# A two-layer attention and expert kernel: score maxima run 44 units ahead in place of 64 (28 of 40 in layer 2)

## The chip, the cores and the metric

The kernel runs on one core of a Trainium2 chip. The metric is the device time of one execution in microseconds (us). A core has TensorE (PE, matmuls, with PEld for its weight loads), VectorE (DVE), ScalarE (ACT), GpSimd (POOL) and SyncE (SP, which here only issues DMAs). Each works through its own instructions in order and waits on semaphores for the others. Instructions and DMAs named here are those of the kernel's own names: `q_strip`, `k_rows`, `a_shift` and so on.

## What is computed

Two layers, each attention times a gate from a mixture of experts, over 8 batches of 512 tokens with 128 features:

```python
xn = _layernorm(x)
s = _L0_attn_ref(xn, ...)          # 16 heads of size 8, full softmax, feed-forward, layer norms
g = _silu(_L0_ffn_ref(xn, ...))    # 16 experts, one per token
x = x + s * g
xn = _layernorm(x)
s = _L1_attn_ref(xn, ...)          # 16 heads of size 8, causal, ALiBi bias
g = _silu(_L1_ffn_ref(xn, ...))    # 8 experts, two per token
x = x + s * g
```

The attention of a batch is a softmax over 512 keys for each of 16 heads and 512 queries: the row maximum is needed before the exponentials.

## The kernel before, in words

The text calls the layers 1 and 2; the code numbers them 0 and 1. There are 16 streams (batch 0 to 7 in layer 1, then batch 0 to 7 in layer 2), and the program is a sequence of **passes** numbered by the stream whose scores they compute, from -2 to 16. `plan(b)` writes out the steps of pass b once, and each of the five engines walks the same list and does its own part of every step. So the place of a step in the list is its place in every engine's queue.

**Units.** A pass consists of 64 units in layer 1 and 40 in layer 2. Unit u of pass b has two halves of work:

- a score unit of stream b: PE multiplies `k_strip` by `q_strip` (L583) into one of three banks, and ACT takes the exponential (L772, L774, L776). In layer 2 two mask matmuls come behind (L540, L541);
- a maximum unit of stream b+1: PE multiplies the other way round (L590) into one of three other banks (four in pass -1, which has no scores), and DVE reduces each row to its negated maximum (L877; in layer 2 L883, with the mask).

All maxima of stream b+1 are computed in pass b, that is a whole pass ahead. When half of them are done, the step `minus` (DVE, L905, L906) splits them into two bf16 parts, and the step `shift` brings them to where the scores need them: PE turns them (L684), ACT copies them to `a_shift` (L795), and SP writes them with four DMAs into two rows of `q_strip` (L511), so that the score matmul subtracts the maximum by itself. PE waits for these DMAs (`shift_in`) before the first score unit of either half: unit 0 and unit 32 in layer 1, unit 0 and unit 20 in layer 2.

**Places.** Between the units stand 32 places, and the tables `MISC`, `LAST0` and `EXTRA` say which other steps stand at which. The second number is the stream relative to b. `("q", 2)` and `("k", 2)` project queries and keys of stream b+2: PE (L669), ACT (L813), four POOL operations that split into three bf16 parts (L1024 to L1027), and then six DMAs on SP to `q_rows` or `k_rows` in DRAM (L482). `("fetch", 2, 0)` loads half of them back into the strips (SP, L494) and waits till the writes have landed. `load` and `loadx` are single loads on SP. `norm`, `onT`, `proj`, `yT`, `logits`, `ff1` and others use PE and the one bank for miscellaneous work; each waits till the step before it has emptied that bank (`claim`). `send0` (in `EXTRA`) writes an eighth of the tokens to the experts of layer 1: four indirect DMAs of POOL (L1662), and each `send0` but the first waits till the one before it has landed. `positions` (POOL, L1426 to L1429) stands behind the last of them.

**Experts.** Between pass 0 and pass 1 stand the experts of layer 1, between pass 9 and pass 10 those of layer 2. SP issues the loads for the first ones only after it has seen `positions`, and their token tiles after all `send0` have landed. The tables `routed` and `sends` fill the passes 5 to 9 with the routing of layer 2, much of it on POOL.

Of the kernel before, what the change touches and what calls it, by code (L numbers as in the profile page):

```python
# [17 lines left out]
QT = S // P  # L18
# [117 lines left out]
UNITS = (H * QT, 10 * QUADS)  # L136
PLACES = 32
# [18 lines left out]
    27: [("ln2", -1), ("gz", -1)], 29: [], 30: [("mix", -1)],  # L156
# [34 lines left out]
def routed(g, choose, count, ends, slots, weigh, table):  # L191
# [65 lines left out]
def plan(b):  # L257


    def live(d):  # L260
        return 0 <= b + d < STREAM

    def layer(d):
        return min(b + d, STREAM - 1) // NB

    steps = []
# [25 lines left out]
    maxima = UNITS[layer(1)] if live(1) else 0  # L292
    units = max(scores, maxima)
# [20 lines left out]
    for u in range(units):  # L314
        si = u if u < scores else None
        mi = u * maxima // units if maxima and (u + 1) * maxima // units > u * maxima // units else None
        if maxima == units:
            mi = u
        steps.append(("unit", 0, (si, mi, layer(1)), layer(0)))
# [1795 lines left out]
```

## Time and profile before

| | us |
|---|---|
| median of 3 runs | 1193.96 |
| the runs | 1193.96, 1189.53, 4205.56 |
| the profiled execution, its own time | 1191.96 |
| its span, first to last instruction | 1190.1 |
| PE busy | 1013.1 (85%) |
| DVE busy | 791.7 (67%) |
| ACT busy | 646.8 (54%) |
| POOL busy | 578.1 (49%) |

PE time is that of matmuls that overlap, with modelled ends, so 85% is not PE at its peak. The granted clock of TensorE over the span is 0.92 of full.

### The profile page before, as it was taken

To read this page: it belongs to the slowest core of one execution; us is meant where nothing else is said; L and a number is where in the kernel's file an instruction comes from. 1 tells how busy PE (TensorE), PEld (TensorE's weight loads), DVE (VectorE), ACT (ScalarE), POOL (GpSimd) and SP (SyncE) were. 2 spreads that over 40 slices of the span, in tenths; PEclk is the share of its full clock that TensorE was granted. 3 is DMA by queue.
4 is the path that set the end of the run, shared out by engine and by line. 5 is a ranking of instruction groups with operands and counts; after the bars stand their busy time and mean duration, and the time that the engine had idled before them with its cause. 6 is when DMAs were issued, how large, how long until landed. Compare 5 with 4: busy or idle time off the path is not lost. (4 is left out here: it accounts for less than half of the span.)

```text
span 1190.1 us, 22919 instructions
## 1 busy us (share of the span) xinstructions
PE 1013.1 (85%) x7466; PEld 543.2 (46%) x7466; DVE 791.7 (67%) x2466; ACT 646.8 (54%) x1252; POOL 578.1 (49%) x670
## 2 busy tenths in 40 slices
PE   4878899999989898878788577777999899899797
PEld 2612279433434333323333244444889654445443
DVE  5597833678787888887765555765444477788641
ACT  1204732576667776656566344444444466677575
POOL 5276400337464655547677576743000155545564
PEclk8667999999999999988999787877999999999889
DMA  5853566733223232303324033233888644454321
GB/s 144 217 146 80 136 169 200 223 102 91 54 56 88 46 98 47 89 5 87 82 66 98 12 74 92 50 85 115 241 242 252 162 108 111 83 135 110 68 56 45
DMA packets 121864, 129.81 MB, mean 109 GB/s; under 512 B 13920, under 2 KB 104864, under 8 KB 121536
## 3 DMA queue, kind: packets, MB, share of 16 engines
q1 hardware_dynamic: 115184, 115.37, 37.4%
q0 software_dynamic: 6144, 12.60, 4.0%
q8 instruction: 58, 0.95, 0.4%
q10 hardware_dynamic: 432, 0.52, 0.2%
q14 instruction: 46, 0.38, 0.1%
HBM read 82.54 MB, written 52.35 MB: 113 GB/s over the span
## 5 line engine op out<-in xcount | busy, mean ns | idle before, releaser
L877 DVE TENSOR_REDUCE a_neg_max<-ps_banks 128x1 f32<-128x512 f32 x512 | 322.7, 681 | 74.5 <-PE ps_banks L590 66.4
L772 ACT ACTIVATE a_probs<-ps_banks 128x512 f32<-128x512 f32 x512 | 278.3, 599 | 143.1 <-PE ps_banks L583 138.4
L583 PE MATMUL ps_banks<-q_strip,k_strip 53*128 53x512 bf16 (+3 forms) x1024 | 281.0, 355 | 72.1 <-DVE a_neg_max L877 31.5
L590 PE MATMUL ps_banks<-k_strip,q_strip 51*128 51x512 bf16 (+3 forms) x1024 | 301.5, 363 | 24.5 <-DVE a_neg_max L883 11.8
L883 DVE CUSTOM_DVE_ANT_0 a_masked<-ps_banks,mask_wide 128x384 bf16<-128x384 f32 (+3 forms) x512 | 224.0, 487 | 90.3 <-PE ps_banks L590 74.6
L774 ACT ACTIVATE a_probs<-ps_banks 128x512 f32<-128x512 f32 x256 | 144.2, 600 | 81.2 <-PE ps_banks L541 72.1
L1067 POOL DMA_INDIRECT tokens<-made,at x96 | 93.6, 975 | 175.6 <-DMA made<-work 124.8
L583 PEld LDWEIGHTS ps_banks<-q_strip,k_strip 53*128 53x128 bf16 x1024 | 72.2, 95 | 161.9 <-issue 54.4
L624 PE MATMUL ps_banks<-a_probs,v_aug 128*32 128x512 f32 x1024 | 141.4, 625 | 0.5 <-ACT a_o_strip L779 0.2
L590 PEld LDWEIGHTS ps_banks<-k_strip,q_strip 51*128 51x128 bf16 x1024 | 74.4, 95 | 142.9 <-ACT a_probs L772 58.7
L2000 POOL DMA_INDIRECT sent<-xn,at x64 | 62.6, 978 | 54.7 <-DMA sent<-xn,at 24.4
L540 PE MATMUL ps_banks<-mask_kq,ident_halves 64*128 64x256 bf16 (+1 forms) x320 | 80.6, 264 | 0.3 <-issue 0.3
L1799 PE MATMUL ps_banks<-work 128*128 128x256 f32 x312 | 76.6, 389 | 1.3 <-DMA work<-in_pack 1.1
L1982 DVE SCALAR_TENSOR_TENSOR work<-ps_banks,work 128x256 f32<-128x256 f32 x78 | 34.2, 479 | 64.0 <-ACT work L1836 55.8
L629 PE MATMUL ps_banks<-a_probs,v_aug 128*32 128x512 f32 (+2 forms) x768 | 76.3, 505 | 0.1
L541 PE MATMUL ps_banks<-mask_kq,ident_halves 64*128 64x128 bf16 (+1 forms) x320 | 66.4, 213 | 0.0
L1024 POOL CAST a_q_parts<-a_q_whole 128x512 bf16<-128x512 f32 x16 | 9.8, 612 | 115.5 <-ACT a_q_whole L813 115.5
L1836 ACT ACTIVATE work<-ps_banks,work 128x256 f32<-128x256 f32 x78 | 32.8, 471 | 56.1 <-PE ps_banks L1799 56.1
L1799 PEld LDWEIGHTS ps_banks<-work 128*128 128x128 f32 x312 | 57.3, 194 | 8.6 <-DMA work<-in_pack 1.8
L776 ACT ACTIVATE a_probs_c<-ps_banks 128x512 f32<-128x512 f32 x64 | 36.4, 595 | 27.9 <-PE ps_banks L541 21.2
L635 PE MATMUL ps_banks<-consts,a_o_strip 128*128 128x128 f32 x252 | 43.1, 296 | 2.5 <-ACT work L817 1.3
L910 DVE RECIPROCAL a_o_den<-ps_banks 128x16 f32<-128x16 f32 x63 | 16.1, 255 | 42.9 <-PE ps_banks L635 40.1
(258 smaller groups left out, 1709.0 us busy)
## 6 DMA issues: line engine op xcount, KB each, us to landing
work<-in_pack SPq DMA_DIRECT2D x39, 450.0 KB, 3.5
q_rows<-a_q_parts SPq DMA_DIRECT2D x96, 128.0 KB
k_rows<-a_k_parts SPq DMA_DIRECT2D x96, 128.0 KB
q_strip<-q_rows SPq DMA_DIRECT2D x64, 192.0 KB
k_strip<-k_rows SPq DMA_DIRECT2D x64, 192.0 KB
work<-in_w SPq DMA_DIRECT2D x32, 256.0 KB, 3.1
sent<-in_zeros SPq DMA_DIRECT2D x14, 512.0 KB, 8.1
work<-sent SPq DMA_DIRECT2D x55, 128.0 KB, 3.3
```

The source lines that it names most:

```text
L540: return pe.matmul(blocks, half_ident(j, half), triangle, start=False, stop=last)
L541: return pe.matmul(blocks[:, :, to], half_ident(j, half), triangle[:, :, src], start=False, stop=last)
L583: mm = pe.matmul(sbank[:, at:at + hi - lo], k_now[rows(js, ROW_END), slot, kt * P:(kt + 1) * P], q_now[rows(js, ROW_END), slot, lo:hi], st ...
L590: mm = pe.matmul(mbank[:, at:at + hi - lo], q_next[rows(jm, ROW_SHIFT), slot, qt * P:(qt + 1) * P], k_next[rows(jm, ROW_SHIFT), slot, lo:h ...
L624: mm = pe.matmul(out_of[c], v_of[k][c], probs[group % 2][:, c, :], start=k == 0, stop=k == QT - 1)
L629: mm = pe.matmul(out_of[c][:, lo:S], v_of[kt][c], kept[:, c, at:at + S - lo], start=kt == 0, stop=kt == 2)
L772: act.activation(probs[si // 4 % 2][:, si % 4, :], bank, ACT.Exp).then_inc(sems["probs"], 1)
L774: act.activation(probs[e // 4][:, e % 4, :], bank, ACT.Exp).then_inc(sems["probs"], 1)
L877: dve.tensor_reduce(neg_max[:, half, qt, hd:hd + 1], bank, AX.X, ALU.max, negate=True).then_inc(sems["max_out"], 1)
L883: op = dve.tensor_tensor_reduce(masked[:, n.at("max_in") % 2, at:at + hi - lo], bank[:, at:at + hi - lo], const["mask_wide"][:, S - (hi - ...
L1067: pool.indirect_dma_start(rows[:, t, :], None, moe[layer], bass.IndirectOffsetOnAxis(ap=routes[layer]["at"][i][:, QT * at + t:QT * at + t ...
L1799: mm = pe.matmul(hidden_bank(par, i)[:, c, :], pack[par][:, (i * FC1 + c) * P:(i * FC1 + c + 1) * P], rows_T[par][:], start=True, stop=True)
```

## The change

Of a stream only the first 44 maxima units (28 in layer 2) are computed in the pass before. The other 20 (12) stand in the stream's own pass, in its first 20 (12) units, next to its scores of the first half; the maxima of the next stream follow behind them. So a pass in the middle of a layer has as many units of each kind as before. Pass -1 has 44 maxima units, not 64. Pass 7, the last of layer 1, has 20 of layer 1 and 28 of layer 2 (before: 40 of layer 2). Pass 15 has 12, before none. `minus` for the second half moves with them, from the end of the pass before to behind unit 19 (11 in layer 2). Both `shift` steps and the `send0` steps get other places.

```diff
+LEAD = (44, 28)
 MISC = {
-    0: {0: [("zTa", 2)], 1: [("ln3a", -2), ("zT", 2)], 2: [("shift", 0, 1)], 3: [("ln3b", -2), ("norm", -1, QT - 1)], 4: [("q", 2)],
+    0: {0: [("zTa", 2)], 1: [("ln3a", -2), ("zT", 2)], 3: [("ln3b", -2), ("norm", -1, QT - 1)], 4: [("q", 2)],
...
-        22: [("shift", 1, 0)], 23: [("gate", -1), ("ff2a", -1)], 24: [("ff2", -1)], 25: [("tanh", -1), ("fmom", -1, 0)], 26: [("fmom", -1, 1)],
-        27: [("ln2", -1), ("norm", 0, 2), ("gz", -1)], 29: [("mix", -1)], 31: [("store", -1)]},
-    1: {0: [("zT", 2)], 2: [("shift", 0, 1)], 4: [("norm", -1, QT - 1)], 6: [("q", 2)], 8: [("k", 2)], 9: [("onT", -1)],
-        11: [("v", 1)], 13: [("norm", 0, 0)], 15: [("proj", -1)], 18: [("fetch", 2, 0)], 19: [("shift", 1, 0)], 21: [("norm", 0, 1)],
+        23: [("gate", -1), ("ff2a", -1)], 24: [("ff2", -1)], 25: [("tanh", -1), ("fmom", -1, 0)], 26: [("fmom", -1, 1)],
+        27: [("shift", 1, 0), ("ln2", -1), ("norm", 0, 2), ("gz", -1)], 29: [("mix", -1)], 31: [("store", -1)]},
+    1: {0: [("zT", 2)], 4: [("norm", -1, QT - 1)], 6: [("q", 2)], 8: [("k", 2)], 9: [("onT", -1)],
+        11: [("v", 1)], 12: [("shift", 0, 1)], 13: [("norm", 0, 0)], 15: [("proj", -1)], 18: [("fetch", 2, 0)], 26: [("shift", 1, 0)], 21: [("norm", 0, 1)],
...
 EXTRA = {
...
-         18: [("send0", 0, 0)], 22: [("send0", 0, 1)], 26: [("send0", 0, 2)], 30: [("send0", 0, 3)]},
-    0: {2: [("send0", 0, 4)], 10: [("send0", 0, 5)], 14: [("send0", 0, 6)], 18: [("send0", 0, 7)], 26: [("positions", 0)]},
+         20: [("send0", 0, 0)], 28: [("send0", 0, 1)]},
+    0: {2: [("send0", 0, 2)], 7: [("send0", 0, 3)], 13: [("send0", 0, 4)], 16: [("send0", 0, 5)], 19: [("send0", 0, 6)], 22: [("send0", 0, 7)],
+        26: [("positions", 0)]},
...
     scores = UNITS[layer(0)] if live(0) else 0
-    maxima = UNITS[layer(1)] if live(1) else 0
-    units = max(scores, maxima)
+    own = [(0, m) for m in range(LEAD[layer(0)], UNITS[layer(0)])] if live(0) else []
+    ahead = [(1, m) for m in range(LEAD[layer(1)])] if live(1) else []
+    units = max(scores, len(own) + len(ahead))
```

In layer 1 the second half's `shift` goes from place 2 to place 11 (the diff leaves that line out), the first half's of the next stream from 22 to 27. Written out as units: in layer 1 from behind unit 4 to behind unit 22, and from 44 to 54; in layer 2 from 3 to 16, and from 24 to 33.

**SP in pass 10**, a pass of layer 2, from the shift of the second half on. Before:

```order
L511 DMA q_strip<-a_shift 1x4x512 [waits a_misc_free]
L511 DMA q_strip<-a_shift 1x4x512 x3
L482 DMA q_rows<-a_q_parts 16x8x512 [waits a_split,a_strips1]
L482 DMA q_rows<-a_q_parts 16x8x512 x5
L482 DMA k_rows<-a_k_parts 16x8x512 [waits a_split,a_strips1]
L482 DMA k_rows<-a_k_parts 16x8x512 x5
L476 DMA work<-x 128x4x128 [waits a_x2_out,a_x2]
L494 DMA q_strip<-q_rows 48x2048 [waits a_scores,a_k_out,a_q_out]
```

Now:

```order
L487 DMA q_rows<-a_q_parts 16x8x512 [waits a_split,a_strips1]
L487 DMA q_rows<-a_q_parts 16x8x512 x5
L487 DMA k_rows<-a_k_parts 16x8x512 [waits a_split,a_strips1]
L487 DMA k_rows<-a_k_parts 16x8x512 x5
L481 DMA work<-x 128x4x128 [waits a_x2_out,a_x2]
L516 DMA q_strip<-a_shift 1x4x512 [waits a_misc_free]
L516 DMA q_strip<-a_shift 1x4x512 x3
L499 DMA q_strip<-q_rows 48x2048 [waits a_scores,a_k_out,a_q_out]
```

The four DMAs of the shift stood ahead of the twelve of queries and keys, and now stand behind them and behind the load of `x`. In layer 1 it is the same, with the load of `a_z_in` in the place of that of `x`.

**PE in the same pass, now**, from the shift (behind unit 16) to unit 20, which is the first score unit of the second half; L589 are scores, L596 maxima, L545 and L546 the masks, L690 the shift, L641 and L716 other steps:

```order
L690 MATMUL ps_banks<-ident_bf,a_minus 16x128 [waits a_misc_free,a_minus]
L690 MATMUL ps_banks<-ident_bf,a_minus 16x128 x3
L589 MATMUL ps_banks<-q_strip,k_strip 128x384 [waits a_max_out,a_probs]
...
L641 MATMUL ps_banks<-consts,a_o_strip 128x128 [waits a_misc_free,a_taken]
...
L589 MATMUL ps_banks<-q_strip,k_strip 128x256 [waits a_max_out,a_probs]
...
L716 MATMUL ps_banks<-wo,a_o_T 128x128 [waits a_misc_free]
L716 MATMUL ps_banks<-wo,a_o_T 128x128 x3
L589 MATMUL ps_banks<-q_strip,k_strip 128x512 [waits a_max_out,a_probs,a_shift_in]
```

Before, sixteen units lay between the two ends of this piece; now there are three.

**POOL in the passes -1 and 0**, from the first of the 32 indirect DMAs of `send0` to `positions`. Before:

```order
L1662 DMA sent<-tokens,at 8192x128 x20
L1024 CAST a_q_parts<-a_q_whole 128x512
L1025 TENSOR_TENSOR a_rest<-a_q_whole,a_q_parts 128x512
L1026 CAST a_q_parts<-a_rest 128x512
L1027 TENSOR_TENSOR a_q_parts<-a_rest,a_q_parts 128x512
L1024 CAST a_k_parts<-a_k_whole 128x512
L1025 TENSOR_TENSOR a_rest<-a_k_whole,a_k_parts 128x512
L1026 CAST a_k_parts<-a_rest 128x512
L1027 TENSOR_TENSOR a_k_parts<-a_rest,a_k_parts 128x512
L1662 DMA sent<-tokens,at 8192x128 x12
L1426 CAST n_pos_parts<-work 16x512
```

Now:

```order
L1668 DMA sent<-tokens,at 8192x128 x12
L1030 CAST a_q_parts<-a_q_whole 128x512
L1031 TENSOR_TENSOR a_rest<-a_q_whole,a_q_parts 128x512
L1032 CAST a_q_parts<-a_rest 128x512
L1033 TENSOR_TENSOR a_q_parts<-a_rest,a_q_parts 128x512
L1030 CAST a_k_parts<-a_k_whole 128x512
L1031 TENSOR_TENSOR a_rest<-a_k_whole,a_k_parts 128x512
L1032 CAST a_k_parts<-a_rest 128x512
L1033 TENSOR_TENSOR a_k_parts<-a_rest,a_k_parts 128x512
L1668 DMA sent<-tokens,at 8192x128 x20
L1432 CAST n_pos_parts<-work 16x512
```

Two of the eight `send0` have moved from ahead of the queries and keys of pass 0 to behind them.

## Rows read from the trace of the kernel before

**Rows 1.** Windows: stretch and its us, busy us per engine, PEclk, DMA share, GB/s.
```profile
46.90:97.30 50.40, 37.57 (x105) 10.57 (x104) 49.41 (x93) 4.70 (x7) 28.97 (x33) 0.67 0.61 174
339.50:400.60 61.10, 56.44 (x392) 23.32 (x388) 50.09 (x114) 43.06 (x82) 33.01 (x36) 1.00 0.32 71
1060.20:1098.50 38.30, 35.06 (x399) 18.99 (x395) 31.27 (x142) 27.47 (x53) 20.65 (x22) 1.00 0.45 113
```

**Rows 2.** Timeline of DVE in pass -1: start, us, instruction, count.
```profile
80.25 16.82 DVE L877 TENSOR_REDUCE a_neg_max<-ps_banks 128x1 f32<-128x512 f32 x28
```

**Rows 3.** Timeline of POOL, passes -1 and 0.
```profile
68.64 1.26 POOL L1578 TENSOR_TENSOR a_probs<-a_probs 128x512 f32<-128x512 f32 x1
...
75.30 1.23 POOL L1662 DMA_INDIRECT sent<-tokens,at  x1 [1.66 <-DVE at L1627]
...
117.97 1.02 POOL L1662 DMA_INDIRECT sent<-tokens,at  x1 [0.15 <-issue]
...
133.69 0.96 POOL L1662 DMA_INDIRECT sent<-tokens,at  x1 [3.88 <-DMA sent<-tokens,at]
...
141.03 1.15 POOL L1429 TENSOR_TENSOR n_pos_parts<-work,n_pos_parts 16x512 bf16<-16x512 f32 x1
```

**Rows 4.** Timeline of ACT in pass 0, and of PE at the first expert.
```profile
112.55 0.69 ACT L813 ACTIVATE a_k_whole<-ps_banks,bk 128x512 f32<-128x512 f32 x1
...
153.23 0.41 PE L1525 MATMUL ps_banks<-consts,work 128*128 128x128 f32 x2 [1.46 <-DMA work<-sent]
```

**Rows 5.** Timeline of a shift in pass 2: its PE step and its four DMAs.
```profile
318.55 0.38 PE L684 MATMUL ps_banks<-ident_bf,a_minus 128*16 128x128 bf16 x4 [0.33 <-ACT work L817]
...
319.86 2.54 SPq L511 DMA_DIRECT2D q_strip<-a_shift  x4
```

**Rows 6.** Timeline of SP and of PE at unit 20, pass 13.
```profile
1082.37 3.78 SPq L482 DMA_DIRECT2D k_rows<-a_k_parts  x6
1086.25 0.55 SPq L476 DMA_DIRECT2D work<-x  x1
1088.05 0.31 SPq L494 DMA_DIRECT2D q_strip<-q_rows  x1
...
1083.62 0.39 PE L583 MATMUL ps_banks<-q_strip,k_strip 53*128 53x512 bf16 x1
```

**Rows 7.** Timeline, passes 10 to 12: SP's load of `x`, then PE's unit 20.
```profile
967.35 0.55 SPq L476 DMA_DIRECT2D work<-x  x1
...
1008.37 0.54 SPq L476 DMA_DIRECT2D work<-x  x1
...
1048.35 0.54 SPq L476 DMA_DIRECT2D work<-x  x1
...
966.77 0.39 PE L583 MATMUL ps_banks<-q_strip,k_strip 53*128 53x512 bf16 x1
...
1005.36 0.39 PE L583 MATMUL ps_banks<-q_strip,k_strip 53*128 53x512 bf16 x1
...
1044.88 0.39 PE L583 MATMUL ps_banks<-q_strip,k_strip 53*128 53x512 bf16 x1
```

**Rows 8.** Timeline, pass 1: SP, then PE at the units 31 and 32.
```profile
248.53 0.60 SPq L470 DMA_DIRECT2D a_z_in<-xn  x1
...
243.85 0.60 PE L583 MATMUL ps_banks<-q_strip,k_strip 53*128 53x512 bf16 x2
```

**Rows 9.** Timeline, pass 8: SP's keys, then PE's unit 20.
```profile
715.30 5.42 SPq L482 DMA_DIRECT2D k_rows<-a_k_parts  x6
...
718.17 0.38 PE L583 MATMUL ps_banks<-q_strip,k_strip 53*128 53x512 bf16 x1
```

**Rows 10.** Timeline of DVE in pass 7.
```profile
664.22 0.98 DVE L1912 TENSOR_TENSOR work<-work 128x8 f32<-128x8 f32 x1 [14.53 <-POOL work L1903]
```

**Rows 11.** Windows in pass 7: an idle stretch of PE, and what follows.
```profile
655.00:666.60 11.60, 0.00 (x0) 0.02 (x1) 2.28 (x9) 0.50 (x1) 7.33 (x15) 0.61 0.08 29
666.60:671.00 4.40, 4.39 (x21) 3.73 (x22) 3.97 (x25) 0.60 (x1) 1.57 (x6) 0.50 0.00 2
```

More of the change, by code:

```diff
@@ L155 @@
     **MISC[0], 12: [("gather", -1)], 16: [("fetch", 2, 0)], 17: [("yT", -1)], 18: [("ff1", -1, 0)], 19: [("ff1", -1, 1)], 20: [("ff1", -1, 2)], 21: [("ff1", -1, 3)],
-    27: [("ln2", -1), ("gz", -1)], 29: [], 30: [("mix", -1)],
+    27: [("shift", 1, 0), ("ln2", -1), ("gz", -1)], 29: [], 30: [("mix", -1)],
 }
@@ L315, in plan @@
         si = u if u < scores else None
[L316 to L319, printed above, removed]
+        md, mi = own[u] if u < len(own) else (1, None)
+        if ahead and u >= len(own):
+            at, left = u - len(own), units - len(own)
+            if (at + 1) * len(ahead) // left > at * len(ahead) // left:
+                md, mi = ahead[at * len(ahead) // left]
+        steps.append(("unit", 0, (si, mi, layer(md), md), layer(0)))
         if scores and u - 1 in late and ends_quad(late[u - 1][1], layer(late[u - 1][0])):
@@ L322, in plan @@
             add("take", d, g // (QT if layer(d) == 0 else 3))
-        if mi is not None and (mi + 1) % (maxima // 2) == 0:
-            add("minus", 1, mi // (maxima // 2))
+        if mi is not None and (mi + 1) % (UNITS[layer(md)] // 2) == 0:
+            add("minus", md, mi // (UNITS[layer(md)] // 2))
         if scores and u in late:
             total(*late[u], RING)
-        while place < PLACES and (place + 1) * units <= (u + (2 if scores == maxima == UNITS[0] else 1)) * PLACES:
+        while place < PLACES and (place + 1) * units <= (u + (2 if scores == len(own) + len(ahead) == UNITS[0] else 1)) * PLACES:
             misc(place)
@@ L568, in _ @@
                         if name == "unit":
-                            si, mi, max_layer = arg
-                            q_now, k_now, q_next, k_next = q_strip[par], k_strip[par], q_strip[1 - par], k_strip[1 - par]
+                            si, mi, max_layer, max_d = arg
+                            max_par = (b + max_d) % 2
+                            q_now, k_now, q_next, k_next = q_strip[par], k_strip[par], q_strip[max_par], k_strip[max_par]
                             sbank, mbank = banks[:, n.at("scores") % RING, :], banks[:, MAX_BANK + n.at("max_in") % RING, :]
@@ L869, in _ @@
                         if name == "unit" and arg[1] is not None:
-                            _, mi, max_layer = arg
+                            _, mi, max_layer, _ = arg
                             bank = banks[:, 2 + n.at("max_in") % 4 if b == -1 else MAX_BANK + n.at("max_in") % RING, :]
```

2 lines of the change are left out of this document (1 added, 1 removed).

## The prediction

> **What bounds the kernel now.** I read the windows pass by pass first, to see which engine has no room in which pass. In pass -1 there are no scores: DVE is busy for 49.4 of 50.4 us and PE works at a mean clock of 0.67, so DVE's row maxima set its length. In the middle of a layer PE has the least room: 56.4 of 61.1 us in pass 3, 35.1 of 38.3 in pass 13, at full clock [rows 1]. What PE loses there by waiting is mostly lost. In the passes 6 to 8, where POOL routes layer 2, DVE and with it PE wait for POOL: 14.5 us in one piece in pass 7 [rows 10]. Then I read the timeline of SP, POOL and PE at the places to which the steps move, since the change computes nothing less; it only moves work between queues.
>
> **Pass -1: what is gained.** 28 maxima in a row take 16.82 us, 0.60 each [rows 2]; 20 fewer are 12.0 us of DVE. But DVE also needs POOL's scan of the expert counts for `slots0`. It ends at 69.9 [rows 3], and DVE will be there 9 units (5.4 us) sooner, the scan by my reading of its chain only some 1.3, since three units leave PE's way to the queries ahead of it on POOL. So I let DVE lose about 4, and PE's first score unit, at 97.3 before [rows 1], comes at about 89.4: 7.9 us sooner. With the first shift now 5 units (3 us) ahead of that unit, its DMAs land just then; no further loss.
>
> **Pass 0: where it goes.** The experts start when `positions` is done, which POOL reaches behind all eight `send0`. Before, three of these stood behind the keys of pass 0, now five. ACT delivers the keys 15.9 us into the pass, at 113.2 [rows 4], so now at 105.3; POOL's split takes 3.8, and the fourth `send0` starts at 109.2. Two periods took from 117.97 to 133.69, 7.86 each, because each waits for the landing of the one before. Four periods give 140.6, and from the start of the last to the end of `positions` it was 8.5 us (133.69 to 142.2) [rows 3]: 149.1, against 142.2. The first expert, at 153.2 waiting for its tokens [rows 4], moves to 160.1: **+6.9** in place of -7.9. PE is idle from about 144 on and starts cold: in pass 7, after 11.6 us without a matmul, it worked 4.4 us at clock 0.50 [rows 11], so I charge 2.2 for each such restart. Sum to here **+9.1**. Bounds: if the landings cost nothing, a period is four issues (5.0 us), `positions` is not late, and -7.9 stays; if all periods are like the last (8.5), +12.
>
> **The shifts: the main term.** A shift takes 1.3 us from PE's step to the first of its DMAs and 2.54 for the four [rows 5]. Their landing is not shown; the nearest row is SP's own wait for the landed keys, from 1086.15 to 1088.05, 1.9 us [rows 6]. So it lands 4.4 us after SP turns to it, 5.7 after PE issued it. It now stands on SP behind the DMAs of queries and keys, which wait for POOL's splits of what PE and ACT made in the same pass. In pass 13 the load behind the keys ends at 1086.8; the shift lands at 1091.2; PE was at unit 20 at 1083.6 [rows 6]. PE's queue is in order, so behind that unit everything waits: scores, maxima, and with them DVE and ACT. That is 7.6 us. By the same sum 5.6, 8.0 and 8.4 us in passes 10 to 12 [rows 7]. Together 29.6; I take 0.5 off each, because queries and keys come a little sooner without the shift at unit 3, and add four cold restarts: **+36.4**. Bounds: 16, if only half of each wait is felt; 45, if each restart costs twice as much.
>
> In pass 1 the load of `a_z_in` ends at 249.1, and PE is at unit 32 at about 244.0 [rows 8]; landing at 253.6 makes 9.6, with the restart **+11.8** (bounds 5 and 14). In pass 8 the keys leave SP at 720.7, unit 20 was at 718.2 [rows 9]: 7.0, and in pass 9 perhaps a third of it; POOL works almost without a pause there, so that a part is hidden: **+7** (0 to 12). In passes 6 and 7 the same wait of 4 to 5 us lies in front of the wait for POOL [rows 10], which hides it: 0; without that cover it would be 9. In passes 0 and 2 to 5 nine units (8.6 us at 61.1/64 each) stand between shift and unit 32 against 5.7, and the keys are out in time: 0, at worst 1 each.
>
> A rule of the Trainium skill bears on this. DMA: Bandwidth & Descriptors, Anatomy of one DMA, gives a small transfer a fixed 2 us from issue to semaphore, most of it for the write's receipt, longest where the target is DRAM. The keys go to DRAM, the shift to on-chip memory. From the start of its last issue the 1.9 us above become about 2.5; with 2.0 for the shift each of the seven waits counted here would be 0.5 shorter and the sum 3.5 less. No run here shows it yet.
>
> **Smaller terms.** In layer 1 the moved shift is followed at once by `logits` and by `norm`, which want the bank that ACT must first empty: about 0.9 us of PE each (1.3 less the step's own 0.38) [rows 5], up to twice a pass. PE has small gaps anyway; **+6** for passes 0 to 5 (0 to 10). At the end of a pass of layer 2 the shift for the next stands 6 units ahead of it; with 14.9 us for 20 units [rows 1, 6] that is about 5 against 5.7 or a little more: 0.6 in seven passes, **+4** (0 to 8). Pass 15 gets 12 maxima units, hidden from DVE (idle there) but not from PE, some 2 us, and in passes 14 and 15 only three units lie between shift and unit 20, 1 and 3 us: **+6** (2 to 9). Pass 7 has 8 more maxima; they lie in front of the wait for POOL: 0, otherwise 5.
>
> **Sum.** 9.1 + 36.4 + 11.8 + 7 + 6 + 4 + 6 = 80.3. The profiled execution took 1192.0 (span 1190.1), 2 below the median of the runs shown. 1192.0 + 80.3 = 1272.
>
> **Rivals.**
> - *The stalls are there, but smaller*: PE catches up behind them, the half clock stays away, POOL covers passes 8 and 9. Half of the shift terms (36.4 + 11.8 + 7 gives 27.6) and of the small ones (8), with pass 0 at +5: 1233. For it speaks that PE's 38.3 us of pass 13 hold 3 us of gaps; against it that the wait holds up every engine but POOL at once. Chance 0.17.
> - *Faster: only pass -1 counts.* If the shifts landed before units 20 and 32, and the `send0` chain took no longer, -7.9 and the +6 of pass 15 and the starts would remain: about 1186, or 1182 without the latter. It is decided by one point: the load behind the keys would have to leave SP 5 to 8 us sooner. ACT and POOL would have to deliver that much earlier; nothing in the change does it. Chance 0.05 (of which 0.03 is more than 2% faster if an unseen wait for the early maxima also goes).
> - *Nothing to measure*: the queue bites in pass 1 and pass 8 alone, and pass -1 pays for it: 1192 - 8 + 19 = about 1203. For that the four waits of passes 10 to 13 would have to vanish into gaps that the windows do not show. Chance 0.09.
> - *Worse*: the waits grow by cold restarts that each last longer, and passes 6 and 7 lose their cover, since their steps towards POOL come later as well: 80 + 9 + 5 + 15 = 1301. Chance 0.09.
>
> **Numbers.** The forecast has 0.60. Its own range, from the bounds of its terms not all taken on one side, is 1250 to 1293. With the second case: 1228 to 1298, which leaves out about 2 in 10. A measurement of this kernel tells about 2% (24 us) from no change. Faster 0.03, within 2% 0.11, slower 0.86.
>
> **What would show it.** Unit 0 of pass 0 at about 89, and the first expert's matmul at about 160, behind an idle PE. In passes 10 to 13 one PE gap of 5 to 8 us each at unit 20, released by DMAs of `a_shift`, with SP's shift right behind the load of `x`; one of 9 us in pass 1 at unit 32. Half clock behind each. Passes 6 and 7 as long as before. It is wrong if the first expert starts before 153, if unit 20 waits less than 3 us, or if pass 13 takes under 43 us.

## The result, and the profile after

The kernel after took 1263.26 us (median of 4 runs, 1258.22 to 1267.03), the kernel before 1194.43 (median of 4, one of which took 4205.56): ratio 1.0588, 95% interval 1.0531 to 1.0645. It is slower, as forecast: 1272 was forecast, with a range of 1250 to 1293. Its profiled execution has a span of 1265.1 us, 75.0 more than that of before; by the medians it is 68.8 more.

Both kernels ran once more, on one chip, with a trace each (the second pair): 1.0592 (1.0553 to 1.0631). Below, `c1_before` and `c2_after` are these two traces; the trace of `c2_after` is that of the slowest of its four runs (1275.91, median 1267.71). Stretch by stretch, in us, from one pass's first score unit on PE to the next pass's; the last line is the difference of the spans:

| stretch | forecast | first pair | second pair |
|---|---|---|---|
| start of pass 0 | -7.9 | -5.8 | -8.1 |
| start of pass 1 (experts of layer 1 done) | +9.1 | +9.4 | +6.8 |
| pass 1 | +11.8 | +9.7 | +12.9 |
| passes 2 to 5 | +6 (for 0 to 5) | +12.0 | +15.0 |
| passes 6 and 7 | 0 | -0.4 | +1.0 |
| passes 8 and 9, with experts | +7 | +1.9 | +5.2 |
| passes 10 to 13 | +36.4 | +36.3 | +33.1 |
| passes 14, 15 and tail (and starts) | +10 | +6.0 | +5.7 |
| sum, without the first line | +80.3 | +75.0 | +79.6 |

The windows of after that answer to [rows 1] (stretch and its us, busy us per engine, PEclk, DMA share, GB/s):

```profile
46.90:91.50 44.60, 30.63 (x86) 9.95 (x84) 40.27 (x72) 4.70 (x7) 25.67 (x29) 0.61 0.59 176
362.40:426.10 63.70, 56.40 (x390) 23.36 (x388) 49.21 (x114) 43.40 (x82) 31.34 (x35) 1.00 0.30 68
1119.20:1167.50 48.30, 38.73 (x399) 20.01 (x396) 30.90 (x143) 28.20 (x53) 20.62 (x22) 0.89 0.39 89
```

Pass 13 takes 48.3 us for the work that took 38.3; its clock fell from 1.00 to 0.89. The totals of PE's waits in after name the new one (engine, line, what it waited for: us, times, longest us):

```profile
PE ps_banks L589 <- DMA q_strip<-a_shift: 43.0, 11, 7.2
PE ps_banks L1531 <- DMA work<-sent: 13.3, 1, 13.3
```

Before, PE nowhere waits for that DMA. Pass 13 in the timeline of after, the place of [rows 6]: PE's shift step, ACT's copy, SP, and PE's unit 20:

```profile
1139.88 0.39 PE L690 MATMUL ps_banks<-ident_bf,a_minus 128*16 128x128 bf16 x4
...
1140.31 0.59 ACT L801 ACTIVATE a_shift<-ps_banks 16x512 bf16<-16x512 f32 x1 [0.22 <-PE ps_banks L690]
1140.79 4.47 SPq L487 DMA_DIRECT2D k_rows<-a_k_parts  x6
...
1145.36 0.54 SPq L481 DMA_DIRECT2D work<-x  x1
1145.94 2.53 SPq L516 DMA_DIRECT2D q_strip<-a_shift  x4
...
1149.66 0.61 PE L589 MATMUL ps_banks<-q_strip,k_strip 53*128 53x512 bf16 x1 [6.16 <-DMA q_strip<-a_shift]
```

The copy is done at 1140.9; SP takes it up at 1145.94, 5.0 us later, because keys and `x` stand ahead. Unit 20 begins 30.5 us into the pass, against 23.4. The windows around it (idle, then what follows):

```profile
1138.50:1149.70 11.20, 4.76 (x55) 3.00 (x53) 4.09 (x20) 4.36 (x9) 5.14 (x6) 0.80 0.58 160
1149.70:1154.80 5.10, 5.10 (x42) 1.89 (x44) 2.17 (x10) 1.68 (x3) 0.00 (x0) 0.50 0.00 0
```

PE works 5.1 us at half clock behind the wait. From unit 20 to unit 24 it needs 5.1 us, before 2.8: the 2.3 lost here stand against the 2.2 charged for a restart.

Pass 1, the place of [rows 8]:

```profile
255.93 0.62 SPq L475 DMA_DIRECT2D a_z_in<-xn  x1
256.60 2.60 SPq L516 DMA_DIRECT2D q_strip<-a_shift  x4
...
260.81 0.61 PE L589 MATMUL ps_banks<-q_strip,k_strip 53*128 53x512 bf16 x1 [6.70 <-DMA q_strip<-a_shift]
```

The start of pass 0, SP's four DMAs of the first shift and PE's unit 0:

```profile
87.46 2.64 SPq L516 DMA_DIRECT2D q_strip<-a_shift  x4
...
91.46 0.58 PE L589 MATMUL ps_banks<-q_strip,k_strip 53*128 53x512 bf16 x1 [2.19 <-DMA q_strip<-a_shift]
```

And pass 0, the places of [rows 3, 4]: the first indirect DMA of four of the five `send0` behind the keys, the end of `positions`, SP, PE's first expert:

```profile
110.65 1.01 POOL L1668 DMA_INDIRECT sent<-tokens,at  x1 [0.15 <-issue]
...
118.74 0.96 POOL L1668 DMA_INDIRECT sent<-tokens,at  x1 [3.28 <-DMA sent<-tokens,at]
...
128.72 0.96 POOL L1668 DMA_INDIRECT sent<-tokens,at  x1 [5.24 <-DMA sent<-tokens,at]
...
141.31 0.96 POOL L1668 DMA_INDIRECT sent<-tokens,at  x1 [1.54 <-DMA sent<-tokens,at]
...
148.65 1.14 POOL L1435 TENSOR_TENSOR n_pos_parts<-work,n_pos_parts 16x512 bf16<-16x512 f32 x1
...
149.82 0.31 SPq L1270 DMA_DIRECT2D alibi_rows<-n_pos_parts  x1
...
154.20 8.61 SPq L1492 DMA_DIRECT2D work<-sent  x6
...
160.53 0.66 PE L1531 MATMUL ps_banks<-consts,work 128*128 128x128 f32 x2 [13.27 <-DMA work<-sent]
```

### The profile page after: what moved, and what is told of

The parts are those of the page before. It is cut to its first block, busy times and chain, and to the rows that moved or that the text cites. A ratio compares the mean times of both kernels' runs of the same rounds, so it can differ in the third digit from the quotient of the medians.

```text
span 1265.1 us, 22912 instructions
## 1 busy us (share of the span) xinstructions
PE 1032.8 (82%) x7466; PEld 549.9 (43%) x7466; DVE 791.0 (63%) x2466; ACT 653.5 (52%) x1252; POOL 576.5 (46%) x670
## 4 chain that ended last, share of the span: by engine, by line
PE 45%; POOL 15%; DVE 10%; DMA 9%; SPq 8%; issue 7%; ACT 5%; another core or an unknown queue 1%; POOLq 0%; DVEq 0%; ACTq 0%
PE ps_banks L589 5%; PE ps_banks L635 5%; PE ps_banks L630 5%; PE ps_banks L1805 5%; SPq L487 4%; PE ps_banks L596 3%; DVE a_neg_max L883 3%; PE ps_banks L733 2%; PE ps_banks L1543 2%; PE ps_banks L727 2%; PE ps_banks L1818 2%; PE ps_banks L1557 2%; POOL sent L2006 2%; POOL tokens L1073 2%; SPq L516 2%
## 5 line engine op out<-in xcount | busy, mean ns | idle before, releaser
L589 PE MATMUL ps_banks<-q_strip,k_strip 53*128 53x512 bf16 (+3 forms) x1024 | 292.2, 367 | 109.8 <-DMA q_strip<-a_shift 43.0
L596 PE MATMUL ps_banks<-k_strip,q_strip 51*128 51x512 bf16 (+3 forms) x1024 | 305.8, 371 | 13.4 <-DVE a_neg_max L883 10.5
L589 PEld LDWEIGHTS ps_banks<-q_strip,k_strip 53*128 53x128 bf16 x1024 | 72.9, 97 | 211.0 <-ACT a_probs L778 58.6
L630 PE MATMUL ps_banks<-a_probs,v_aug 128*32 128x512 f32 x1024 | 147.0, 648 | 0.9 <-ACT a_o_strip L785 0.8
L596 PEld LDWEIGHTS ps_banks<-k_strip,q_strip 51*128 51x128 bf16 x1024 | 74.7, 97 | 121.5 <-ACT a_probs L778 56.6
L545 PE MATMUL ps_banks<-mask_kq,ident_halves 64*128 64x256 bf16 (+1 forms) x320 | 83.4, 270 | 0.7 <-issue 0.7
L635 PE MATMUL ps_banks<-a_probs,v_aug 128*32 128x512 f32 (+2 forms) x768 | 80.3, 527 | 0.1
L546 PE MATMUL ps_banks<-mask_kq,ident_halves 64*128 64x128 bf16 (+1 forms) x320 | 67.8, 216 | 0.0
L641 PE MATMUL ps_banks<-consts,a_o_strip 128*128 128x128 f32 x252 | 44.5, 303 | 10.9 <-ACT a_shift L801 7.8
L1122 POOL TENSOR_TENSOR tokens<-tokens,a_resid 128x512 f32<-128x512 f32 x7 | 8.9, 1273 | 87.7 <-ACT a_shift L801 80.1
```

The source lines that it names most:

```text
L545: return pe.matmul(blocks, half_ident(j, half), triangle, start=False, stop=last)
L589: mm = pe.matmul(sbank[:, at:at + hi - lo], k_now[rows(js, ROW_END), slot, kt * P:(kt + 1) * P], q_now[rows(js, ROW_END), slot, lo:hi], st ...
L596: mm = pe.matmul(mbank[:, at:at + hi - lo], q_next[rows(jm, ROW_SHIFT), slot, qt * P:(qt + 1) * P], k_next[rows(jm, ROW_SHIFT), slot, lo:h ...
L630: mm = pe.matmul(out_of[c], v_of[k][c], probs[group % 2][:, c, :], start=k == 0, stop=k == QT - 1)
L635: mm = pe.matmul(out_of[c][:, lo:S], v_of[kt][c], kept[:, c, at:at + S - lo], start=kt == 0, stop=kt == 2)
```

## The experiments

They ran on three chips, called A, B and C here, on which the kernel before took 1196.6, 1174.6 and 1176.4 us. Ratios are to the kernel before on the same chip, as recorded; quotients of the medians differ from them by up to 0.35%. The second pair, `e7_k_behind` and `e8_short` ran on A. Which chip the first pair ran on is not recorded; its times are like those of A, and it is counted with A below. On B and C the kernel after was not run unchanged, and the kernel before has no trace there. In layer 1 the chips do not differ up to where the versions do (unit 20 of the passes 2 to 5 begins 20.8 us into the pass on all three). In passes 10 to 13 B and C agree with each other (unit 17 at 17.0 in `e3_sends` on B and in `e9_positions` on C), and A is later (last section). The diffs below are cut to the entries that change.

| run | chip | median us | ratio, interval |
|---|---|---|---|
| c1_before | A | 1202.40 | 1.0036 (0.9998 to 1.0075) |
| c2_after | A | 1267.71 | 1.0592 (1.0553 to 1.0631) |
| e1_act_queue | B | 1217.05 | 1.0353 (1.0291 to 1.0414) |
| e2_late_only | B | 1238.73 | 1.0519 (1.0457 to 1.0582) |
| e3_sends | B | 1253.24 | 1.0650 (1.0588 to 1.0712) |
| e4_apart | B | 1251.24 | 1.0619 (1.0544 to 1.0694) |
| e7_k_behind | A | 1239.83 | 1.0387 (1.0344 to 1.0430) |
| e8_short | A | 1209.09 | 1.0117 (1.0084 to 1.0150) |
| e9_positions | C | 1247.15 | 1.0616 (1.0569 to 1.0664) |
| e10_first_shift | C | 1247.75 | 1.0603 (1.0547 to 1.0658) |
| e11_best | C | 1178.51 | 1.0028 (1.0003 to 1.0053) |
| e12_sum | C | 1214.04 | 1.0313 (1.0266 to 1.0360) |

**The shift alone.** Before, with only this step moved:

```diff
-        2: [("shift", 0, 1)],
-        11: [("logits", -2)],
+        11: [("shift", 0, 1), ("logits", -2)],
...
-        2: [("shift", 0, 1)],
+        12: [("shift", 0, 1)],
```

> The kernel before with its maxima still a whole pass ahead; only the step that shifts the second half moves to the place it has after the change (from behind unit 4 to behind unit 22 in layer 1, from 3 to 16 in layer 2). Theory (SP's queue): the same waits with nothing else of the change: pass 1 +9.7, passes 10 to 13 about +33, passes 8 and 9 +2, and +1.4 for the bank behind the shift in each of 5 passes: 1192 + 52 = 1244 us (1232 to 1255). Rival (own maxima in the stream's own pass are the cost): no more than 1205, and unit 20 of passes 10 to 13 at 24 us as before.

Measured 1.0519, at the upper end of what I expected (1244 of 1192 is 1.044, 1255 is 1.053). Pass 1 took 70.3 us, passes 10 to 13 47.2, 46.3, 45.6 and 46.2. Pass 13, SP and PE's unit 20:

```profile
1127.69 0.54 SPq L476 DMA_DIRECT2D work<-x  x1
1128.28 2.53 SPq L511 DMA_DIRECT2D q_strip<-a_shift  x4
...
1131.99 0.60 PE L583 MATMUL ps_banks<-q_strip,k_strip 53*128 53x512 bf16 x1 [8.13 <-DMA q_strip<-a_shift]
```

Not one maximum has moved here, and the same wait stands at the same unit. The rival, that the maxima in the stream's own pass are the cost, falls. The passes 10 to 13 take 143.6 us together with layer 2 as before (`e11_best`, C), 185.3 here (B), and 189.6, 193.4 and 190.7 with layer 2 as after (`e3_sends` and `e4_apart` on B, `e9_positions` on C). Taking B and C as alike, 42 of 46 to 50 us come with this one step.

**The queue alone.** After, in SP's part only: the keys' six DMAs behind the shift's four.

```diff
-                        if name in ("q", "k"):
+                        behind = b == 1 or NB <= b <= STREAM - 3
+                        if name == "q" or name == "k" and not behind:
...
+                        if name == "shift" and arg == 1 and behind:
+                            wait(sp, sems["split"], n.at("split"))
+                            for a in range(PARTS):
+                                sp.dma_start(dram["k"][par][:, a, :, :],
...
```

> The kernel after; in pass 1 and in layer 2, SP alone issues the six DMAs of the keys behind the four of the second half's shift, not ahead of them. Nothing moves on any other engine. Theory (the queue's order is the cause): the shift leaves SP behind the queries, at 21.8 + 2.6 = 24.4 us into the passes 10 to 13 and lands at 25.7, 4.5 sooner; in pass 1 at 30.8, landing at 32.3, 4.7 sooner. 5 passes by 4.6 and 1 each for the passes 8 and 9: 25 us less than the kernel after (20 to 28). Rival 1 (the keys, now late, hold up the load of the strips and with it the next pass's unit 0): no gain, every pass 5 us late at its start. Rival 2 (what holds unit 20 up is the work of the stream's own maxima): no gain.

Measured 1.0387 against 1.0592 on the same chip: by the ratios 24.5 us less, by the medians 27.9, expected 25. Pass 13:

```profile
1118.50 5.14 SPq L488 DMA_DIRECT2D q_rows<-a_q_parts  x6
1123.74 0.54 SPq L481 DMA_DIRECT2D work<-x  x1
1124.32 2.53 SPq L517 DMA_DIRECT2D q_strip<-a_shift  x4
1126.94 3.78 SPq L523 DMA_DIRECT2D k_rows<-a_k_parts  x6
...
1128.01 0.39 PE L596 MATMUL ps_banks<-q_strip,k_strip 53*128 53x512 bf16 x1 [2.62 <-DMA q_strip<-a_shift]
```

The wait fell from 6.47 in pass 13 of `c2_after` (6.16 in after) to 2.62, and the matmul behind it takes 0.39 in place of 0.61: here the clock did not fall. In passes 10 and 11 it still did, behind waits of 2.34 and 2.06. PE's waits for the shift were 20.9 us in all, against 43.4 in `c2_after`. Passes 10 to 13 took 169.1 us; after 192.2, before 159.1. That the keys now left late (rival 1) cost nothing that shows. With no step moved on another engine, this shows the order of SP's queue to be the cause. What remains is the shift's wait behind the six DMAs of the queries and the load of `x`.

**Another queue.** After, with the shift's DMAs issued by ACT behind its own copy:

```diff
                             act.activation(shift[:], ps_misc[0:2 * NG, :], ACT.Copy).then_inc(sems["misc_free"], 1)
+                            wait(act, sems["misc_free"], n.at("misc_free") + 1)
+                            for j in range(2):
+                                for a in range(2):
...
+                                    act.dma_start(q_strip[par][r:r + 1, arg * QT:(arg + 1) * QT, :],
...
```

> The kernel after, but ACT issues the four DMAs of each shift right behind its own copy; SP issues none. Theory (the shift waits on SP behind queries and keys): pass 1 falls back from 70.2 to about 60.5 us; in passes 10 to 13 the shift lands 1.3 + 2.5 + 1.5 = 5.3 us after PE's step at 20.5 us into the pass, where unit 20 would be at 24: some 2 us of wait stay, passes of about 42 instead of 48.5. Passes 8 and 9 give 2. In all 1263 - 10 - 26 - 2 = 1225 us (1215 to 1238). Rival 1 (the split of the maxima over two passes costs the time, by a worse balance of PE, DVE and ACT): 1250 or more, and unit 20 still late. Rival 2 (ACT, held for 2.5 us by each shift, becomes the new wait): unit 20 lands, but the exponentials behind the shift are 2.5 us late each time, 1240.

Measured 1.0353: near the upper end of what I had expected (1.017 to 1.037 of the kernel before, most likely 1.026). Passes 10 to 13 took 157.7 us, 32 and 36 less than with the shift in SP's queue on the same chip (189.6 in `e3_sends`, 193.4 in `e4_apart`), where I had expected 26. In layer 1 it gave little: pass 1 took 65.2, not 60.5, and passes 2 to 4 69.1, 65.4 and 66.4, no less than after. ACT's timeline, here in pass 13, shows what a shift costs there:

```profile
1100.29 2.52 ACTq L799 DMA_DIRECT2D q_strip<-a_shift  x4
1102.86 0.60 ACT L773 ACTIVATE a_probs<-ps_banks 128x512 f32<-128x512 f32 x1 [2.60 <-issue]
```

ACT issues for 2.5 us and computes nothing. In PE's waits, those for the exponentials of layer 1 grow to 21.9 us (after: 13.9). Theory and rival 2 both hold: the wait shrinks (to 15.4 us in all, from 64.0 in `e3_sends` on this chip), and a smaller one takes its place.

**The sends.** After, with `send0` at its places of before:

```diff
-         20: [("send0", 0, 0)], 28: [("send0", 0, 1)]},
-    0: {2: [("send0", 0, 2)], 7: [("send0", 0, 3)], 13: [("send0", 0, 4)], 16: [("send0", 0, 5)], 19: [("send0", 0, 6)], 22: [("send0", 0, 7)],
+         18: [("send0", 0, 0)], 22: [("send0", 0, 1)], 26: [("send0", 0, 2)], 30: [("send0", 0, 3)]},
+    0: {2: [("send0", 0, 4)], 10: [("send0", 0, 5)], 14: [("send0", 0, 6)], 18: [("send0", 0, 7)],
```

> The kernel after with the send0 steps at their old places (four in pass -1, five ahead of the queries of pass 0, three behind the keys). Theory: the two sends that moved behind the keys are two landing periods of 6.3 to 10 us; with three sends there positions ends near 142 instead of 149.8 and the first expert starts near 153 instead of about 161: 1263 - 7 = 1256 us (1251 to 1260). Rival 1 (the chain is set by landings in any order): first expert at 160, 1263. Rival 2: the queries and keys of pass 0, now behind one more send, are late for PE, which starts the experts late from its own work: 1260 or more.

`positions` ended at 142.7, as expected, yet the first expert began only at 158.18, and nothing was gained (1.0650; `e4_apart`, with the sends as in after, has 1.0619 on this chip and its first expert at 156.3). Rival 2 came true: five sends ahead of queries and keys made these late, with them the shift behind them on SP, and PE stood still at unit 32 of pass 0; that made the other shift late on SP:

```profile
126.60 0.61 PE L588 MATMUL ps_banks<-q_strip,k_strip 53*128 53x512 bf16 x1 [7.87 <-DMA q_strip<-a_shift]
```

```profile
144.85 2.43 SPq L515 DMA_DIRECT2D q_strip<-a_shift  x4
147.32 0.44 SPq L1269 DMA_DIRECT2D alibi_rows<-n_pos_parts  x1
```

SP was free for the experts at 147.3, though `positions` was done 4.6 us earlier. So by this trace the new places of the sends spare that wait in pass 0, at a price of about the same size.

**The chain before the experts.** After, with `positions` ahead of `send0` 5:

```diff
-        26: [("positions", 0)]},
+        15: [("positions", 0)],
```

> The kernel after with the step positions (3.7 us of POOL) moved from behind the last send0 to ahead of send0 5, where POOL stands idle for 3 to 5 us until a send has landed. Theory (the chain POOL, positions, SP's loads of the weights, tokens sets the first expert): SP goes on right behind its shift at 52.1 us into pass 0 in place of 58.1, and the first expert starts some 5 us sooner, at about 155 in place of 159.4 to 160.5: 5 us less than the kernel after, ratio about 1.055. Rival (the landing of the last send sets it, positions is hidden): no change, 1.059. In both PE still starts the experts at half clock.

In the trace the first expert began at 148.41, 58.8 us behind unit 0 of its pass, against 69.1 in after and 65.8 in `e4_apart`, whose sends stand at the same places. The chain of sends starts 15.9 us ahead of unit 0 here and 16.0 in `e4_apart`; of the 10 us against after, 3 are thus not the gain of this step. Now the landing of the last send ends the wait: SP had the weights issued at 140.6 and took the tokens at 146.23.

```profile
139.85 0.71 SPq L1488 DMA_DIRECT2D work<-in_w  x1
...
146.23 3.24 SPq L1491 DMA_DIRECT2D work<-sent  x5
...
148.41 0.66 PE L1530 MATMUL ps_banks<-consts,work 128*128 128x128 f32 x2 [8.66 <-DMA work<-sent]
```

So the theory holds in the trace. The ratio, 1.0616 in place of the 1.055 that I expected, does not show 5 us: it is no lower than the 1.0619 of `e4_apart`, and these intervals reach 0.5 and 0.75% to either side.

**The ends of the passes in layer 1.** These lost twice what I had forecast. First try: the first half's shift away from the step `norm`, whose bank it holds.

```diff
-        27: [("shift", 1, 0), ("ln2", -1), ("norm", 0, 2), ("gz", -1)],
+        27: [("ln2", -1), ("norm", 0, 2), ("gz", -1)], 28: [("shift", 1, 0)],
```

> The kernel after with the first half's shift of layer 1 one place later, two units behind the norm step and not directly ahead of it. Theory (the shift's bank must be emptied by ACT before norm can use it): about 0.8 us less in each of the passes 1 to 6, and what builds on it: 1263 - 5 = 1258 us (1254 to 1262). Rival (the end of the pass is long because the shift lands late for the next pass's unit 0): each of these passes 2 us longer, since the shift is 2 units later: 1273. Third (both nothing): 1263.

Passes 2 to 5 took 67.8, 65.2, 65.2 and 74.1 us: 272.4 against 272.2 and 275.4 in the two traces of after. The third case, nothing. (The unchanged kernel, with which this compares, ran on A.) The windows of `c2_after` in pass 3 show what I had left out, the shift and what follows it, and then the stretch behind:

```profile
420.00:424.40 4.40, 2.84 (x24) 1.08 (x22) 4.05 (x12) 2.77 (x7) 2.68 (x4) 1.00 0.01 2
424.40:427.80 3.40, 2.99 (x14) 0.62 (x16) 2.06 (x4) 1.01 (x2) 3.24 (x5) 0.53 0.01 2
```

with two of three short waits of PE in and just ahead of the first (the third is one of 0.86, ahead of 419.86):

```profile
422.22 0.63 PE L641 MATMUL ps_banks<-consts,a_o_strip 128*128 128x128 f32 x4 [0.77 <-ACT a_shift L801]
...
424.81 0.58 PE L589 MATMUL ps_banks<-q_strip,k_strip 53*128 53x512 bf16 x1 [1.21 <-ACT a_probs L778]
```

Waits of about 1 us, close together, were followed by 3.4 us at clock 0.53. In `e4_apart` the waits are others, but the half clock is there too (0.51 from 418.4 to 421.4). The Trainium skill (TensorE: Matmul & The Clock Gate, A second HAM failure mode: psum-queue depth-cycling) describes such a swing from short idle gaps between groups of matmuls; this trace agrees. What decides whether it happens is not shown: at the same place of `c1_before` PE waits 0.86 and 1.32 us, 4 us apart, and the clock stays at 1.00. Second try: the maxima 54 ahead, so that the step can stand at its old place.

```diff
-LEAD = (44, 28)
+LEAD = (54, 28)
...
+        22: [("shift", 1, 0)],
...
-        27: [("shift", 1, 0), ("ln2", -1), ("norm", 0, 2), ("gz", -1)],
+        27: [("ln2", -1), ("norm", 0, 2), ("gz", -1)],
```

> The kernel after with maxima 54 in place of 44 units ahead in layer 1, so that the first half's shift can stand at its old place (behind unit 44, not 54); the second half's stays behind unit 22. To be read in the passes 2 to 5, which lasted 68.4, 65.0, 66.2 and 75.8 us in the kernel after and 64.4, 61.6, 61.6 and 72.8 in that before on the same chip. Theory (the late first shift, wedged between the end of the maxima, norm and the exponentials, makes gaps of 0.8 to 1.2 us in a row behind which the clock falls to a half): the ends lose it, only the 1.3 at unit 22 stays, 65.7, 62.9, 62.9, 74: 10 us less in four passes. Pass -1 is 6 us longer, and with five sends behind the keys the first expert about 5 later, so the total is only some 5 us below the kernel after, 1.055. Rival (it is the maxima of two streams in one pass that cost there): the passes stay at 65 to 68.

Passes 2 to 5 took 63.6, 62.1, 63.2 and 73.3: 262.2 us, 10 less than in `e4_apart` and `e9_positions` (272.4, 272.0). The end of pass 3 in a window, at full clock throughout:

```profile
412.00:419.90 7.90, 6.18 (x48) 1.62 (x47) 7.73 (x18) 4.96 (x10) 6.75 (x8) 1.00 0.00 0
```

The maxima of two streams still share these passes, though 10 units of a stream's own and not 20. Two other rows say that they are not the cost: `e2_late_only`, where none has moved, takes the same 262.4 us, and in after the passes 2 to 5 are no later than before up to unit 22, where the 20 own maxima stand. The late first shift is. The total (1.0603, expected 1.055) shows none of it, since the first expert began at 160.13, in `e4_apart` at 156.3: the later keys push the sends, as expected.

**A short lead.** After, with 4 units in the own pass and every step at its place of before, but for the shift of the second half in layer 2, which stands one unit later (so at unit 4 in both layers, ahead of the queries):

```diff
-LEAD = (44, 28)
+LEAD = (60, 36)
```

> The kernel after with maxima 60 (36) units ahead, so that only 4 units stand in the stream's own pass; the shift of the second half is then possible ahead of the queries on every queue, at unit 4. The other shift and send0 at their places of before. Theory: no wait at unit 20 or 32, no bank wait: as before within 5 us; pass -1 is 2.4 us shorter, which the send0 chain takes back. Ratio 1.000 (0.995 to 1.005). Rival 1 (splitting the maxima costs by itself): 1.01 or more. Rival 2 (faster: pass 0 starts 2.4 us sooner and PE, not the chain, sets the first expert): 0.997.

Measured 1.0117, outside what I expected; rival 1 has the number. Waits for `a_shift` are gone, but PE's shift step now stands one unit behind `minus`:

```profile
PE ps_banks L689 <- DVE a_minus L911: 26.4, 20, 3.4
```

26.4 us in 20 places. In layer 1 the passes take most of it back (passes 2 to 4: 64.6, 61.8, 61.8, `c1_before` 64.4, 61.6, 61.6); passes 10 to 13 took 166.3 against 159.1. Pass 0 began 3.7 us sooner than in `c1_before`, the first expert only 1.9, at half clock, and pass 1 not at all.

**Both kernels to be beaten.** Three units in the own pass in layer 1, layer 2 as before, `positions` ahead of the last send; shown against the kernel before:

```diff
+LEAD = (61, 40)
...
-        20: [("ff1", -1, 2)], 21: [("ff1", -1, 3)], 22: [("shift", 1, 0)],
+        20: [("shift", 1, 0)], 21: [("ff1", -1, 2)], 22: [("ff1", -1, 3)],
...
-        26: [("positions", 0)]},
+        17: [("positions", 0)],
```

> A version that could beat both: maxima 61 units ahead in layer 1 (three in the own pass, the shift at unit 4 ahead of the queries), layer 2 all as before, send0 as before, positions ahead of the last send0, the first half's shift of layer 1 behind unit 40 in place of 44. Theory: pass -1 2 us shorter, SP reaches the expert loads 3 us sooner, nothing lost in the passes: 0.997 (0.993 to 1.001), at the edge of what can be measured. Rival (the passes 1 to 7 lose 0.7 each by the shift that waits for the early maxima, as in the version with 60): 1.001 or more.

Measured 1.0028 (1.0003 to 1.0053): not better, and the rival's number. The first expert began at 149.91, at full clock, and pass 1 at 211.1 (before 214.4 and 216.3 on A), but passes 1 to 5 took 330.2 us, before 320.7 and 321.3. The gain was given back there, mostly in the second half of the passes: in pass 2 unit 20 begins at 21.0 (before 20.8), unit 36 at 34.8 (33.9), the last at 67.6 (64.3). I did not find which of its moves does that.

**The sum.** After, with the edits of `e7_k_behind`, `e10_first_shift` and `e3_sends` at once, and one more:

```diff
-        26: [("positions", 0)]},
+        17: [("positions", 0)],
```

> The kernel after with four things put right at once: keys behind the shift on SP (pass 1, layer 2), first shift of layer 1 at its old place (54 units ahead), send0 as before, positions ahead of the last send0. If the terms add: pass 0 and the first expert as before, pass 1 +6, passes 2 to 6 +1.3 each, passes 8 to 13 +11, 14 and 15 +1: 1197 + 24 = 1221, ratio 1.020 (1.014 to 1.027). Rival (the terms share waits, and where one goes another takes its place): 1.030 or more.

Measured 1.0313, above the range. The first expert began at 153.19, pass 1 took 66.4 us, passes 2 to 4 63.6, 62.1 and 63.0, as expected or shorter. Passes 10 to 13 did not: 173.9 us, 17 less than in `e9_positions` but 30 more than the 143.6 of `e11_best`, where I had put 11. That 11 came from chip A, where these passes begin late by themselves (last section): in both `e7_k_behind` on A and `e12_sum` on C unit 20 begins 25.0 to 27.5 us into the pass, but with layer 2 as before it begins at 23.4 to 26.3 on A and 19.8 to 21.2 on C. That accounts for the miss in these passes. The ratio is the rival's (1.030 or more); its reason, that one wait takes the place of another, these rows do not show.

For comparison the two controls.

> The kernel before, unchanged, to have its trace from the same chip as those of the experiments. In the experiments so far unit 17 of the passes 10 to 13 began 17.0 us into the pass, in the first trace of before 20.5 to 22.8, with PE held up by nothing that the trace names. Theory (that was a thing of the execution or of the chip): 17.0 here too, and 1175 us. Rival (the early place of the shift makes it): 20.5 or more. Pass 0 to first expert 153, pass 1 60.5.

The trace came from another chip than those it was to be compared with. Unit 17 of passes 10 to 13 began at 21.3, 20.8, 22.4 and 23.4. On C, with the shift as early as here, it is 16.9 to 18.3 (`e11_best`), and on A with the shift late 20.6 to 20.9 (`c2_after`). So it belongs to the chip, as the theory allowed, and not to the shift's place. The first expert began at 155.11, pass 1 took 60.8.

> The kernel after, unchanged, on the same chip. Theory: the ratio to before is 1.059 again, 1244 us beside 1175; unit 20 of passes 10 to 13 at about 30, 9 us behind that of before. Rival (the chip on which the experiments ran bears the waits worse): 1.065 or more.

1.0592, unit 20 at 30.1, 30.6, 29.7 and 30.5. Against the 1202.40 of `c1_before` alone, the medians give 1.0543. Whether B and C bear the waits worse was not measured on the unchanged kernel; `e3_sends`, `e4_apart` and `e9_positions` with 1.062 to 1.065 speak for it.

## Why the prediction was right, and where it was not

The forecast of 1272 was 9 us above the median of 1263.26; in the traces +80.3 stands against +75.0 and +79.6. The signs that it named were there: the first expert at 160.53, the waits for `a_shift` at unit 20 and unit 32 with the shift right behind the load, half clock behind them, passes 6 and 7 as before. That the sum came so near is in part luck: the passes 2 to 5 cost 6 to 9 us more than the term for 0 to 5, and the passes 8, 9, 14 and 15 together 6 to 9 less.

**Pass -1 (-7.9).** Measured -5.8 and -8.1. The first send began at 76.03, before at 75.30 [rows 3]: the scan and what follows it did not come sooner. Even so PE was done with the maxima at 89.27, 8.0 us before unit 0 of the kernel before. Then unit 0 waited 2.19 us for the DMAs of the first shift (2.23 in `c2_after`), a wait that the prediction had put at nothing ("its DMAs land just then").

**Pass 0 (+9.1).** Right by its mechanism. The fourth send began at 110.65 (forecast 109.2), four periods took 30.7 us (31.4), from the start of the last to the end of `positions` 8.5 (8.5). The first expert began at 160.53 and 159.41 (160.1). The restart cost 2.1 and 2.5 (2.2): from first expert to pass 1 it took 63.3 and 63.7, before 61.2 in both. `e9_positions` shows the chain; `e3_sends` shows what I did not see, that the queries and keys, and SP's two shifts, stand in this chain as well.

**The shifts in passes 10 to 13 (+36.4).** Right: +36.3 and +33.1, and shown by `e2_late_only` and `e7_k_behind`. The parts differ somewhat. The shift landed sooner than 1.9 us behind SP's four issues; in pass 13 it was 1.2 (1148.47 to 1149.66). Taken from the start of that last issue, some 0.6 earlier, it is 1.8, and in pass 1 2.2. The Trainium skill (DMA: Bandwidth & Descriptors, Anatomy of one DMA) gives 2. It says so of DMAs that GpSimd issues, and these are SP's; the trace agrees with it better than with my row of the keys (2.5 on the same count), and the correction that I had set beside the sum was due. The restart was 2.3 in pass 13 in place of 2.2. About 0.6 us a pass in these four, between units 31 and 39, belongs to the term for the pass starts. On chip C layer 2 as after costs 47 us in these passes.

**Pass 1 (+11.8).** Measured +9.7 and +12.9. Unit 32 came sooner in the first pair (at 37.0 us, forecast 39.2): with no shift at unit 4 SP finished the load of `a_z_in` 2 us sooner, which I had allowed for in layer 2 and not here.

**Passes 2 to 5 (in the +6).** The term that was mis-sized most: +12.0 and +15.0. I had taken ACT's turn at the bank twice a pass and read the clock only for long waits. From unit 22 to 23 it took 1.4 more, the cost that I had in mind. Most of the rest came from the end of the pass: short waits in a row and half clock, in pass 2 of `c2_after` 0.50 from 352.9 to 363.0. `e10_first_shift` took 10 us of it away.

**Passes 6 and 7 (0).** Right, -0.4 and +1.0: the wait for the shift hides in front of that for POOL. In pass 7 unit 32, which waits for the shift, comes 8.3 us later (37.6 us into the pass in place of 29.3), and the pass is only 1.3 longer.

**Passes 8 and 9 (+7).** Too high: +1.9 and +5.2. Unit 20 of pass 8 did come 5.0 us later, but unit 31 came 0.4 us sooner than before (in the second pair 5.3 and 0.8 later): the wait was nearly wholly hidden, where I had counted on a part.

**Pass starts, 14 and 15 (+10).** +6.0 and +5.7 in the passes 14 and 15, and the 0.6 a pass above. The term for the starts has a slip: six units of 14.9/20 us are 4.5, not about 5, so by its own working it is 8, not 4. That 0.6 a pass came out after all is luck.

The faster rival fell by the point that it named, the load behind the keys: it left SP at 26.7 us into pass 13 (before 26.6), not 5 to 8 us sooner. Its time was added up wrongly: 1192.0 - 7.9 + 6 is 1190, and 1184 without the 6, not 1186 and 1182. "Smaller stalls" fell by the half clock, which is there behind the waits of 4.7 to 7.7 us in pass 1 and the passes 10 to 13 of both traces of after; behind those of 1.0 to 1.6 us in passes 14 and 15 it is not.

## What to carry to other kernels

Before a step is moved, list for each queue what it will stand behind, and when that is ready: four DMAs of 4 KB cost 33 to 36 us of a kernel because twelve others, for a stream two passes ahead, and a load stood in front; putting six of them behind gave some 25 us back. A step that shortens a prologue is worth only what the next chain lets through; here 6 to 8 us ended in a chain that was already the bound, and two sends more in that chain made it longer. Count gaps of 1 us on TensorE where several stand close together; behind them the clock fell in pass 3 of `c2_after` as behind one long gap.

## What the runs showed of the hardware

**The chips differ in one kind of stretch.** In passes 10 to 13 with layer 2 as before, unit 11 begins 10.3 to 11.7 us into the pass on chip C and 12.9 to 16.8 on chip A, in both traces of before. With the shift late it is 10.2 to 10.3 on B and C and 12.0 to 14.4 on A. Chip A, `c1_before`, then chip C, `e11_best`, the first eleven units of pass 13:

```profile
1062.80:1079.60 16.80, 12.67 (x125) 6.17 (x120) 10.29 (x47) 9.12 (x17) 8.25 (x10) 0.90 0.32 83
```

```profile
1050.50:1060.80 10.30, 10.30 (x126) 5.45 (x122) 9.82 (x47) 8.88 (x17) 3.86 (x5) 1.00 0.52 109
```

PE computes the same matmuls (125 and 126); on A 6.5 us pass besides. The trace names no engine and no DMA of the kernel for the wait from which the longest of these gaps stems:

```profile
1074.68 0.26 DVE L910 RECIPROCAL a_o_den<-ps_banks 128x16 f32<-128x16 f32 x1 [2.16 <-remote]
```

What it is stays open. It matters for reading: on A part of the wait for the shift hides behind it. With the shift late, unit 20 begins 29.6 to 31.0 us into the pass on C and 29.7 to 32.0 on A, but before the change 19.8 to 21.2 and 23.4 to 26.3, so the same change costs 33 to 36 us in these passes on A and 47 on C.

**The length of a wait does not decide alone what the clock does behind it.** In `e7_k_behind` the granted clock was 0.50 in the 3 us behind a wait of 2.34 us in pass 10, and 1.00 behind one of 2.62 in pass 13. What decides it stays open.

**The landings of indirect DMAs vary.** The period from one `send0` to the next, where no other work lay between, was 6.3 to 10.0 us for the same four DMAs, within the one execution of after.
